# Mixture-of-experts up projection: one float32 product replaced by three float32r products of high and low parts

## What is computed

```python
for e in range(E):                      # 8 experts
    w1 = w13[e, :FFN]                   # 512 x 256
    w3 = w13[e, FFN:]                   # 512 x 256
    g = jax.nn.silu(h @ w1.T) * (h @ w3.T)
    out = out + jnp.einsum('tf,hf->th', g, w2[e]) * wfull[:, e:e + 1]
```

## Time and profile before

| | us |
|---|---|
| median of 3 runs | 2653.84 |
| lowest and highest run | 2651.22 and 2654.06 |
| time of the profiled execution | 2649.78 |
| its span in the profile | 2647.9 |
| of that, `after` (about 2012 to 2203) | 191 |
| of that, `experts` (2203 to the end) | 445 |

### The profile page before, as it was taken

How to read it: one execution, slowest core, us unless ns; L and a number is a source line. 1 busy time by engine, 2 the same in 40 slices (tenths; PEclk the granted TensorE clock), 3 DMA queues, 4 the chain that set the end, 5 groups by cost and what they waited for, 6 DMA issues and landing times. The chain is left out here.

```text
span 2647.9 us, 51768 instructions
## 1 busy us (share of the span) xinstructions
PE 2386.8 (90%) x17986; PEld 1218.3 (46%) x17987; DVE 1886.0 (71%) x3954; ACT 1502.3 (57%) x3282; POOL 548.0 (21%) x824
## 2 busy tenths in 40 slices
PE   3299976999999999999999999999996866999997
PEld 2155543444444444444444444444443643666664
DVE  6767757899998998999998999999971762222221
ACT  2033311787787777778787778777784531222221
POOL 4411100111111111111111111111000462222222
PEclk9599985999999999999999999999998987999999
DMA  4167773843543443322332232231014852333333
GB/s 151 60 171 209 216 183 55 129 77 65 82 76 71 76 76 77 59 56 51 62 57 53 56 60 54 52 60 51 24 40 154 294 189 54 68 70 66 68 69 62
DMA packets 167494, 238.60 MB, mean 90 GB/s; under 512 B 52068, under 2 KB 126964, under 8 KB 161232
## 3 DMA queue, kind: packets, MB, share of 16 engines
q0 software_dynamic: 37328, 107.98, 21.8%
q1 hardware_dynamic: 127136, 127.58, 17.1%
q10 hardware_dynamic: 2816, 0.16, 0.1%
HBM read 112.24 MB, written 122.36 MB: 89 GB/s over the span
## 5 line engine op out<-in xcount | busy, mean ns | idle before, releaser
L1410 DVE TENSOR_REDUCE a_mx<-banks 128x1 f32<-128x512 f32 (+3 forms) x2560 | 1378.7, 602 | 153.0 <-PE banks L1214 78.9
L1366 ACT ACTIVATE a_p<-banks 128x512 f32<-128x512 f32 (+3 forms) x2560 | 1177.3, 540 | 319.3 <-PE banks L1229 198.5
L1329 PE MATMUL banks<-a_p,a_v 128*32 128x512 f32 (+3 forms) x5120 | 600.6, 544 | 1.0 <-ACT a_p L1366 0.5
L1214 PE MATMUL banks<-a_k,a_q 48*128 48x512 f32 (+7 forms) x1600 | 340.4, 429 | 9.9 <-DVE a_mx L1410 1.9
L1229 PE MATMUL banks<-a_q,a_k 50*128 50x512 f32 (+7 forms) x1600 | 331.9, 426 | 11.2 <-ACT a_p L1366 4.6
L1964 PE MATMUL banks<-w,e_hT 128*128 x576 | 261.9, 598 | 1.5 <-ACT e_hT L2021 1.5
L1214 PEld LDWEIGHTS banks<-a_k,a_q 52*128 52x128 f32 (+1 forms) x1600 | 155.1, 185 | 209.6 <-DVE a_mx L1410 164.9
L1229 PEld LDWEIGHTS banks<-a_q,a_k 54*128 54x128 f32 (+1 forms) x1600 | 152.4, 184 | 199.9 <-DVE a_mx L1410 144.7
L2066 DVE TENSOR_TENSOR e_g<-e_silu,banks 128x512 f32<-128x512 f32 x72 | 49.5, 687 | 272.3 <-ACT e_silu L2027 272.3
L1214 PE MATMUL banks<-a_k,q 52*128 52x512 f32 (+7 forms) x944 | 215.1, 459 | 27.3 <-DMA a_k<-aug_rows 14.4
L2021 ACT ACTIVATE e_hT<-banks 128x256 f32<-128x256 f32 x72 | 27.7, 384 | 342.9 <-PE banks L1953 342.9
(11 more groups left out here) (251 smaller groups left out, 2225.8 us busy)
## 6 DMA issues: line engine op xcount, KB each, us to landing
expert_rows<-a_zeros POOLq DMA_DIRECT2D x132, 258.0 KB, 5.3
e_x<-expert_rows SPq DMA_DIRECT2D x72, 129.0 KB, 3.0
a_k<-ka_parts POOLq DMA_DIRECT2D x36, 256.0 KB, 6.3
expert_rows<-e_y SPq DMA_DIRECT2D x72, 128.0 KB, 2.1
qa_parts<-m_part SPq DMA_DIRECT2D x16, 512.0 KB, 4.4
ka_parts<-m_part SPq DMA_DIRECT2D x16, 512.0 KB, 4.9
va_tiles<-m_va SPq DMA_DIRECT2D x8, 1024.0 KB, 5.0
qb_parts<-m_part SPq DMA_DIRECT2D x16, 512.0 KB, 4.7
```

Of the source, the lines that this page charges most:

```text
L1214: ins = pe.matmul(outs[j][:, 0:w], q_op[o][part, p, qt * P:(qt + 1) * P], (keys or k_op[o])[part, kp, k0:k0 + w], start=True, stop=not dia ...
L1329: ins = pe.matmul(ps_o[VW * h:VW * h + VW, c0:QB], v_op[o][:, kt, hk * VW:hk * VW + VW], prob[:, (n * GH + h) % NPB, c0:QB], start=(kt == ...
L1366: nc.scalar.activation(prob[:, (2 * n + j) % NPB, c0:QB], ps[(slot + j) % RING][:, c0:QB], ACT.Exp, scale=SCALE).then_inc(s_ex, 1)
L1410: v.tensor_reduce(mx[:, j, p, qt, k0 // WIDE:k0 // WIDE + 1], ps[banks[j]][:, 0:w], AX.X, ALU.max).then_inc(s_md, 1)
```

## The change

In `after`, the 8 weight matrices `w13` are turned into their float32r high parts in place by ACT, one activation of 128 x 2048 elements for each expert (`high(e)`), placed between the copies and the exponentials of a block. From expert 2 on, SP waits for `high(e-2)` before it issues the load of expert e. Two semaphores are merged to make room.

In `experts`, ACT first issues 8 loads of 1024 KB that bring the raw `w13` once more from HBM, into the new tile `e_w13low`. DVE subtracts the high parts in place for experts 0 and 1 (4 operations of 128 x 1024), and POOL for experts 2 to 7 (12 operations), each before its other work. For each tile ACT's copy writes a float32r high part of the turned rows, and a new DVE operation `low_rows(n)` subtracts it from the PSUM bank to give the low part. `up(n)` is then 12 float32r products of 512 columns: for each k, high rows by high weights, high rows by low weights, low rows by high weights, each for the gate and the up part. It also waits for the low weights of its expert (`s_low`).

```diff
@@ after, SyncE @@
             def expert(e):
-                sp.dma_start(M["w13"][:, e * KD:(e + 1) * KD, :], w13_d[:, e, :, :]).then_inc(M["s_w13"], 16)
+                if e >= 2:
+                    sp.wait_ge(M["s_high"], e - 1)
+                sp.dma_start(M["w13"][:, e * KD:(e + 1) * KD, :].bitcast(F32), w13_d[:, e, :, :]
+                             ).then_inc(M["s_w13"][e % 2], 16)
@@ after, ScalarE @@
+            def high(e):
+
+                own = M["w13"][:, e * KD:(e + 1) * KD, :]
+                act.wait_ge(M["s_w13"][e % 2], e // 2 * 16 + 16)
+                sc.activation(own, own.bitcast(F32), ACT.Copy).then_inc(M["s_high"], 1)
...
                 if n + 1 < NBLK:
                     turned(n + 1)
                 if n >= 1:
+                    high(n - 1)
+                if n >= 1:
                     odds_of(n - 1)
...
             odds_of(NBLK - 1)
+            high(NE - 1)
@@ experts, tiles @@
-        hT = [sb(f"e_hT{s}", [P, KD, P]) for s in range(2)]
+        hT = [[sb(f"e_hT{c}{s}", [P, KD, P], F32R) for s in range(2)] for c in range(2)]
+        low = sb("e_w13low", [P, NE * KD, 2 * FFN], F32R)
...
+        OWN_LOW = 2
@@ experts, GpSimd @@
             pool.sem_inc(s_ok, R)
+            pool.wait_ge(s_low, OWN_LOW * KD)
+            for i in range(OWN_LOW * KD, NE * KD):
+                pool.wait_ge(s_raw[i // KD], RAW[i // KD])
+                nc.gpsimd.tensor_tensor(low[:, i, :], low[:, i, :].bitcast(F32), w13[:, i, :].bitcast(F32),
+                                        ALU.subtract).then_inc(s_low, 1)
@@ experts, TensorE, up @@
-                for part, bank in enumerate((ps_g[s], ps_u[s])):
-                    for k in range(KD):
-                        ins = pe.matmul(bank[:, :], hT[s][:, k, :],
-                                        w13[:, ds(e * KD + k, 1), part * FFN:(part + 1) * FFN].rearrange(
-                                            "p o m -> p (o m)"), start=(k == 0), stop=(k == KD - 1))
+                pe.wait_ge(s_low, e * KD + KD)
+                for k in range(KD):
+                    for c, of in ((0, w13), (0, low), (1, w13)):
+                        for part, bank in enumerate((ps_g[s], ps_u[s])):
+                            ins = pe.matmul(bank[:, :], hT[c][s][:, k, :],
+                                            of[:, ds(e * KD + k, 1), part * FFN:(part + 1) * FFN].rearrange(
+                                                "p o m -> p (o m)"), start=(k == 0 and c == 0 and of is w13),
+                                            stop=(k == KD - 1 and c == 1))
@@ experts, ScalarE @@
-            act.sem_inc(s_hT, AHEAD)
+            for e in range(NE):
+                act.dma_start(low[:, e * KD:(e + 1) * KD, :].bitcast(F32), w13_d[:, e, :, :]).then_inc(s_raw[e], 16)
@@ experts, VectorE @@
+            def low_rows(n, s):
+
+                dve.wait_ge(s_hi, n + 1)
+                high = hT[0][s][:, :, :].rearrange("p k t -> p (k t)").bitcast(F32)
+                v.tensor_tensor(hT[1][s][:, :, :].rearrange("p k t -> p (k t)"), ps_h[:, 0:D], high,
+                                ALU.subtract).then_inc(s_hT, 1)
...
+            for i in range(OWN_LOW * KD):
+                dve.wait_ge(s_raw[i // KD], RAW[i // KD])
+                v.tensor_tensor(low[:, i, :], low[:, i, :].bitcast(F32), w13[:, i, :].bitcast(F32),
+                                ALU.subtract).then_inc(s_low, 1)
+            low_rows(0, 0)
+            tags(0, 0, 0, 0)
+            low_rows(1, 1)
+            tags(0, 1, 1, 1)
             for n in range(2):
-                tags(0, n, n, n)
                 product(n, n)
+                low_rows(n + 2, n)
             with dve.Fori(0, NTILES // R - 1) as i:
                 for o in range(R):
                     n = i * R + (o + 2)
                     tags(i * 2 + (o + 2) // 2, n, o % 2, (o + 2) % R)
                     product(n, o % 2)
+                    low_rows(n + 2, o % 2)
                     result(i, i * R + o, o)
```

More of the change, by code:

```diff
@@ L1576, in _ @@
             g.memset(ones[:, :], 1.0).then_inc(s_one, 1)
-            g.memset(lgT[:, :], 0.0).then_inc(s_z, 1)
+            g.memset(lgT[:, :], 0.0).then_inc(s_one, 1)
             def scatter(n):
@@ L1664, in _ @@
             pe.wait_ge(s_w, 80)
-            pe.wait_ge(s_z, 1)
+            pe.wait_ge(s_one, 2)
             front(0)
@@ L1671, in _ @@
                     pe.wait_ge(s_k, 7 * 16)
-                    pe.wait_ge(s_one, 1)
+                    pe.wait_ge(s_one, 2)
                 if n >= 1:
@@ L1873, in experts @@
         s_tag = sem("exp_tokens_kept")
-        s_ht, s_hT = sem("exp_rows_turned"), sem("exp_hT_ready")
+        s_ht, s_hi, s_hT = sem("exp_rows_turned"), sem("exp_hT_high_ready"), sem("exp_hT_ready")
+        s_raw, s_low = M["s_moved"], sem("exp_w13_low_ready")
+        RAW = [M["moved"][e] + 16 for e in range(NE)]
+        w13_d = A["w13"].rearrange("e (k p) m -> p e k m", p=P)
         s_up, s_si, s_g = sem("exp_up_ready"), sem("exp_silu_ready"), sem("exp_product_ready")
@@ L1879, in experts @@
         s_add, s_ok = sem("exp_results_added"), sem("exp_addition_landed")
[L1880 removed]
+        s_last, s_first = sem("exp_first_rows_gathered"), sem("exp_first_rows_summed_then_stored")
+        SUMMED, STORED = 2, 18
         AHEAD = 2
+        OWN_LOW = 2
         hs_d = M["hs_d"].rearrange("(n p) d -> p n d", p=P)
@@ L1913, in _ @@
                 store(n, n % R)
-            sp.wait_ge(s_sum, 2)
+            sp.wait_ge(s_first, SUMMED)
             sp.wait_ge(s_add, NTILES * 16)
-            sp.dma_start(out[0:P, :], sum0[:, :]).then_inc(s_out, 16)
-            sp.wait_ge(s_out, 16)
+            sp.dma_start(out[0:P, :], sum0[:, :]).then_inc(s_first, 16)
+            sp.wait_ge(s_first, STORED)
         @block.gpsimd
@@ L1941, in _ @@
             pe.sem_inc(s_dn, AHEAD)
-            pe.wait_ge(M["s_w13"], NE * 16)
+            pe.wait_ge(M["s_high"], NE)
             pe.wait_ge(M["s_w2"], NE * 16)
@@ L2020, in rows @@
                 act.wait_ge(s_up, n + 1)
-                nc.scalar.activation(hT[s][:, :, :].rearrange("p k t -> p (k t)"), ps_h[:, 0:D],
-                                     ACT.Copy).then_inc(s_hT, 1)
+                nc.scalar.activation(hT[0][s][:, :, :].rearrange("p k t -> p (k t)"), ps_h[:, 0:D],
+                                     ACT.Copy).then_inc(s_hi, 1)
             def silu(n, s):
@@ L2092, in _ @@
             dve.wait_ge(s_last, 32)
-            v.tensor_tensor(sum0[:, :], last[0][:, 0:D], M["res0"][:, :], ALU.add).then_inc(s_sum, 1)
-            dve.wait_ge(s_sum, 1)
-            v.tensor_tensor(sum0[:, :], sum0[:, :], last[1][:, 0:D], ALU.add).then_inc(s_sum, 1)
+            v.tensor_tensor(sum0[:, :], last[0][:, 0:D], M["res0"][:, :], ALU.add).then_inc(s_first, 1)
+            dve.wait_ge(s_first, 1)
+            v.tensor_tensor(sum0[:, :], sum0[:, :], last[1][:, 0:D], ALU.add).then_inc(s_first, 1)
 def program(nc, A, out):
@@ L2137, in program @@
                 middle(nc, A, M)
+                M["moved"] = [16 + NBLK * 16] * (NBLK - 1) + [16 + NBLK * 32]
             attention(nc, A, M)
@@ L2146, in program @@
         M["tile_rows"] = keep("tile_rows", [P, NTILES], mybir.dt.int32)
-        M["w13"] = keep("w13", [P, NE * KD, 2 * FFN])
+        M["w13"] = keep("w13", [P, NE * KD, 2 * FFN], F32R)
         M["w2"] = keep("w2", [P, NE * FT, D])
-        M["s_w13"], M["s_w2"] = nc.alloc_semaphore("w13_loaded"), nc.alloc_semaphore("w2_loaded")
+        M["s_w13"] = [nc.alloc_semaphore(f"w13_loaded{i}") for i in range(2)]
+        M["s_high"], M["s_w2"] = nc.alloc_semaphore("w13_high_ready"), nc.alloc_semaphore("w2_loaded")
         after(nc, A, M, out)
```

3 lines of the change are left out of this document (2 added, 1 removed).

## The result

The changed kernel takes **2745.3 us** (median of 4 runs, 2744.89 to 2746.79), the kernel before 2653.52 on the same chip (4 runs): ratio 1.035, 95% interval 1.033 to 1.037. The profiled execution spans 2743.1 us against 2647.9.

What follows compares the result with a forecast made beforehand. PE was taken to bound the kernel before, at 5.82 us a slot. Ring 103, start 15 and `after` 2 give 120 us on 2649.8, so 2769.8; 4.1 more for the median makes 2774 us, range 2715 to 2829.

Steps and rivals of the forecast that it cites:

- The ring: Experts' loop: turned rows, subtraction, held result, store, next load and back take 7.34 us a slot, +103 us over 68 slots.
- The start: Start of `experts`: first `up` 8 us late, tile 4 held 7 us by POOL's subtractions, +15 us together.
- `after`: Stage `after`: ACT's 8 added copies of about 1.8 us are mostly covered by idle time, +2 us, between 0 and 5.
- PE's own work: Experts' loop: `up` 2.76, `down` 1.73 and turned rows 0.66 make 5.15 us a slot.
- Only the first wait counts: Rival, experts' loop: rows arrive in time, only `down` waits for the held result; slot 6.51 us, 2718 us, chance 9%.
- PE stays the bound: Rival, experts' loop: low rows find their input ready, so the result is not held; 2625 us, chance 4%.
- The products are slower: Rival, `up`: a float32r product takes 0.43 us on the full array; slot 8.91 us, 2881 us, chance 5%.
- The clock falls: Rival, experts' loop: PE's idling lowers its clock to 1.2 GHz; slot about 11.2 us, 3040 us, chance 4%.
- The rule on short idles: PE in the loop: the skill page reports short idles between matmul groups make the clock go down and up again.
- The queues: Start of `experts`: transfer engines go round queues with work, so SP's rows would not wait behind ACT's weights; otherwise start 25.
- another releaser than `e_y`: Refuting sign, experts' loop: PE's idle before `down`, expected about 1.4 us with `e_y` as cause, names something else.

Runs made afterwards that it cites:

- e3: The kernel before, with one wait added on VectorE that holds each result until the turned rows of tile n+2 are copied: 2732.4 us, ratio 1.031.
- e1: The changed kernel with VectorE's result of tile n-2 put ahead of the subtraction for tile n+2: 2625.5 us, ratio 0.992.
- e2: The changed kernel with the result of tile n-2 and the tags of tile n+1 both ahead of the subtraction for tile n+2: 2615.6 us, ratio 0.987.
- e7: The changed kernel with eight buffers, loads one tile further ahead and tags before the low rows, result still behind them: 2714.3 us, ratio 1.023.
- e4: The changed kernel with 8 instead of 12 products in `up`, leaving out low rows by high weights: 2743.1 us, ratio 1.036.
- e6: e5 with VectorE making low parts of one expert only, and ScalarE issuing two copies before its first rows, six behind: 2616.5 us, ratio 0.987.
- e5: e2 with eight buffers instead of four for results, tokens and weights, and SyncE's stream written out tile by tile: 2622.1 us, ratio 0.988.
- e8: e2 with GpSimd's 12 subtractions put one behind each of its first 12 additions: 2612.5 us, ratio 0.985.
- e10: The changed kernel, its VectorE order kept, with only GpSimd's 12 subtractions put between the first 12 additions: 2742.2 us, ratio 1.035.
- e9: e8 with e6's start, GpSimd making the other 14 subtractions behind its first 14 additions: 2612.2 us, ratio 0.985.

## Why the prediction came out as it did

The sign and the mechanism held: the result was held behind a subtraction whose input is made a slot later, and e3 and e1 show that this order alone brings the slot of 7 us and that taking it away removes it. The size was 120 us for 95. By its terms:

- **The ring**, 7.34 us, measured 7.05: right in its parts and 0.3 too long. In the slot shown it is 7.13: 1.71 from turned rows to the end of the result (2443.64 - 2441.93), 2.17 to the load's issue and 3.25 to the next turned rows. Over 48 slots of the loop the three are 1.75, 2.29 and 2.99, against 1.82, 2.32 and 3.2 in the sum. So most of the excess is the last part: I had added 0.2 us for PE to wake on the landed rows, and it takes 0.05; the landing is 2.95 where I had 3.0. The rest is DVE: the subtraction starts at 2442.82 and the result at 2443.17, so two operations of 0.42 and 0.47 overlap a little, and I had added them up. Over 68 slots the ring is 84 us instead of 103, 19 of the 25 us of error.
- **The start**, 15 us, measured about 10. I had the first `up` 8 us late and it is 5.9, counted from the first load. Two terms were wrong and neither decided it: ACT's 8 issues of a copy took 7.28 us, 0.9 each, where I had taken 1.5 from SP's issues of the same size, and the first rows landed in 6.7 us instead of 2.1. What `up` waited for was DVE's last subtraction of weights, which ended at 2214.81 where the prediction had "near 2215". Tile 4 was held by the mechanism foreseen, but for 3.3 us and not 7: the first addition started at 2243.6 where I had POOL free at 2245, and it had landed by 2247.6 where I had 2250.
- **`after`**, +2 us, measured 1.05 at the first load, which is less than the scatter between executions: with the changed `after` the first load stands anywhere from 2200.2 to 2210.9, with the old one at 2203.5 (e3) and 2204.9. So no run here shows this term, or rules it out. The eight copies took 1.92 us each, where I had 1.8.
- **PE's own work**, 5.15 us. e2's slot is 5.16. Twelve products of float32r lie 0.23 us apart (2446.67 to 2447.60 for four), as the earlier trace rows said of half an array. In e2 `up` takes 2.98 instead of 2.76 and `down` 1.54 instead of 1.73, which is one and the same shift: the first record of `up` starts 0.03 us after the last of `down`, and the second 0.42 after it. The sum hardly moves.
- **The rivals.** *Only the first wait counts* gave 6.51; e7 built that case, and it is 6.70. It wasn't the changed kernel's, where the turned rows wait for the load in every slot. *PE stays the bound* gave 2625 and needed the result not to be held: that is e2, at 2616. *The products are slower* fell with the distance of 0.23. *The clock falls*: it was 1.00 in the loop, with PE idle for 1.3 us of each slot (69 us of 380), most of it ahead of `down`. The rule on short idles that I set against the row (the Trainium skill, TensorE: Matmul & The Clock Gate, "A second HAM failure mode: psum-queue depth-cycling") did not show in this kernel. It may have in e4, where PE has less work: `down` at 3.60 us in one slot, and over 2300 to 2680 us a clock of 0.95:

```profile
2300.00:2680.00 380.00, 273.35 (x1181) 204.16 (x1180) 88.20 (x270) 73.53 (x162) 83.58 (x54) 0.95 0.31 56
```

- **The queues.** That SP's rows would not stand behind ACT's weights, which I drew from the Trainium skill (DMA: Bandwidth & Descriptors, "Queues, rings and completion order"), held only in part: the first rows didn't wait for all 8 MB (each copy landed 13.3 us after its issue in the median), but 6.7 us is 4.6 more than alone.

The profile after names ACT's copy `e_gT` as what `down` waits for, where I had written that another releaser than `e_y` would refute the forecast. Who reads only that would mend the wrong engine. The copy ends at 2443.77, between the result (2443.64) and `down` (2443.90), and so is the last event before it; e1 and e3, which leave ACT alone and move the result, tell them apart.

## What to carry to other kernels

An operation put into an in-order engine's stream brings its wait with it, and everything behind inherits that wait; ask of each added instruction when its input is made, and put behind it nothing that is ready sooner. Here the result, the tags and the low rows in another order turn +3.5% into -1.3%. When a stall goes away and the time stays, look for a serial chain with nearly the same pace as the bound: what it lost at the start it wins back slowly (e6) or not at all (e5), and starting it sooner is the remedy to try.

## What the runs showed of the hardware

- A float32r product of 128 x 128 by 512 columns starts 0.233 us after the last one at full clock, as close as the pairs on half the array; three of them cost 0.70 us, where one float32 product of the kernel before, two records of 0.43, cost 0.86. The three-part product is cheaper by 19%.
- A load of 129 KB landed in a median of 2.1 us in e1, where it is issued ahead of the store and the addition, and in 3.0 where it follows them (changed kernel, e2). Beside eight copies of 1024 KB of another engine's queue the first took 6.4 to 6.9 us (changed kernel, e1, e2, e4, e5, e7, e8, e10). With two copies ahead of it, it still took 6.4 in e6 and 5.5 in e9.
- Additions by indirect transfer, each waiting for the one before it, start 4.4 to 6.1 us apart and 5.13 in the mean (e5): 4.3 us to land and 0.8 until the next starts.
- GpSimd's subtraction of 128 x 1024 took 2.37 us with nothing but others of its kind on GpSimd (changed kernel) and 2.9 to 3.0 between additions (e8).
- ScalarE issues a copy of 1024 KB in 0.9 us at the start of `experts`, and in 0.54 (3.26 / 6) when the transfers are under way (e6).
